# Iterated attention: a Newton step on GpSimd, another VectorE order, and a rearranged end

## What is computed

```python
q, k, v = heads(xn @ Wq + bq), heads(xn @ Wk + bk), heads(xn @ Wv + bv)   # 16 heads of 64
q, k = layernorm(q, gamma, beta), layernorm(k, gamma, beta)               # over the 64 of a head
def step(carry, _):
    q_cur, converged = carry
    attn = softmax(einsum('bhqd,bhkd->bhqk', q_cur, k) / 8)
    out = einsum('bhqk,bhkd->bhqd', attn, v)
    diff = norm(out - q_cur)                  # one number over all of the tensor
    q_new = where(converged, q_cur, out)
    return (q_new, converged | (diff < 1e-4)), None
(q_final, _), _ = scan(step, (q, False), None, length=3)
x = x + merge_heads(q_final) @ Wo + bo + ffn(xn)
```

## Time and profile before

| | us |
|---|---|
| median of 3 runs (lowest, highest) | 3179.82 (3178.55, 3186.2) |
| the profiled execution | 3181.74 |
| its span, first to last instruction | 3180.4 |

### The profile page before, as it was taken

One profiled execution on the slowest core, in us unless ns is written; L12 is line 12 of the kernel. 1 busy time (PEld: TensorE's weight loads), 2 busy tenths in 40 slices (PEclk: granted clock), 3 DMA queues, 4 the chain that ended last, 5 costly groups with the idle time before them and its releaser, 6 DMA issues.

```text
span 3180.4 us, 72036 instructions
## 1 busy us (share of the span) xinstructions
PE 2905.9 (91%) x24663; PEld 2226.7 (70%) x24663; DVE 2526.8 (79%) x5836; ACT 2206.5 (69%) x6152; POOL 2012.5 (63%) x2045
## 2 busy tenths in 40 slices
PE   6999988886999979999979999999999999999997
PEld 4666555565788877897857777777777777777775
DVE  7788899569777764664578888888888888888886
ACT  4566666643555565465368888888888888888885
POOL 2633344223555555235068888888888888888884
PEclk7999999998999989999989999999999999999998
DMA  3222422000000011102000000000000000000000
GB/s 117 73 80 73 147 86 86 19 7 1 1 1 1 1 51 53 35 1 64 2 13 2 2 2 1 2 2 2 2 2 2 2 2 2 2 2 2 1 2 27
DMA packets 68871, 77.15 MB, mean 24 GB/s; under 512 B 8016, under 2 KB 60320, under 8 KB 68384
## 3 DMA queue, kind: packets, MB, share of 16 engines
q1 hardware_dynamic: 64912, 71.10, 7.3%
q10 hardware_dynamic: 3600, 1.46, 0.2%
HBM read 52.61 MB, written 18.87 MB: 22 GB/s over the span
## 4 chain that ended last, share of the span: by engine, by line
PE 38%; DVE 10%; POOL 8%; issue 5%; ACT 4%; DVEq 0%; POOLq 0%; ACTq 0%
PE psum L2562 9%; PE psum L2544 7%; PE psum L2526 6%; POOL attn_p L3024 4%; DVE attn_pt L2823 2%; DVE sb_few L2810 2%; PE psum L1908 2%; PE psum L1759 2%; ACT attn_p L2668 2%; PE psum L2001 2%; PE psum L1761 2%; PE psum L1760 2%; PE psum L2589 2%; PE psum L1808 2%; PE psum L2468 1%
## 5 line engine op out<-in xcount | busy, mean ns | idle before, releaser
L3024 POOL TENSOR_TENSOR attn_p<-attn_p,sb_few 128x512 f32<-128x512 f32 x768 | 797.3, 1052 | 174.1 <-DVE sb_few L2817 172.0
L2668 ACT ACTIVATE attn_p<-psum,sb_few 128x256 f32<-128x256 f32 x1536 | 721.1, 480 | 60.9 <-DVE sb_few L2810 60.8
L2810 DVE TENSOR_REDUCE sb_few<-psum 128x2 f32<-128x512 f32 x768 | 508.5, 680 | 12.1 <-PE psum L2526 6.7
L2544 PE MATMUL psum<-sb_kept,attn_p 128*128 128x128 f32 x3072 | 412.0, 277 | 33.1 <-DVE attn_pt L2823 29.2
L2562 PE MATMUL psum<-attn_pt,attn_v 128*64 128x256 f32 x3072 | 384.2, 387 | 30.7 <-DVE attn_pt L2823 30.7
L2544 PEld LDWEIGHTS psum<-sb_kept,attn_p 128*128 128x128 f32 x3072 | 335.7, 141 | 82.5 <-issue 30.4
L506 DVE TENSOR_REDUCE sb_a_nm<-psum 128x2 f32<-128x512 f32 x512 | 329.0, 685 | 64.9 <-PE psum L396 46.9
L572 ACT ACTIVATE sb_a_pt<-psum 128x512 f32<-128x512 f32 x512 | 278.8, 598 | 93.8 <-PE psum L403 65.5
L2668 ACT ACTIVATION_READ_ACCUMULATOR attn_p<-psum,sb_few 128x1 f32 x1536 | 318.9, 208 | 0.0
L2562 PEld LDWEIGHTS psum<-attn_pt,attn_v 128*64 128x64 f32 x3072 | 202.7, 136 | 156.9 <-issue 75.4
L2823 DVE COPY attn_pt<-psum 128x512 f32<-128x512 f32 x384 | 264.0, 688 | 34.0 <-PE psum L2544 29.8
(11 more groups left out here) (441 smaller groups left out, 7706.8 us busy)
## 6 DMA issues: line engine op xcount, KB each, us to landing
sb_a_spread<-a_spilled SPq DMA_DIRECT2D x64, 256.0 KB, 3.0
a_spilled<-sb_a_part_hi SPq DMA_DIRECT2D x64, 128.0 KB
a_spilled<-sb_a_part_lo SPq DMA_DIRECT2D x64, 128.0 KB
sb_a_spread<-a_spilled SPq DMA_DIRECT2D x64, 128.0 KB, 3.2
sb_gate_up<-in_L_ffn_Wg SPq DMA_DIRECT2D x32, 128.0 KB
sb_gate_up<-in_L_ffn_Wu SPq DMA_DIRECT2D x32, 128.0 KB
sb_down_w<-in_L_ffn_Wd SPq DMA_DIRECT2D x32, 128.0 KB, 2.5
sb_x<-in_L_attn_x SPq DMA_DIRECT2D x4, 512.0 KB, 7.6
```

The source lines that it names most:

```text
L2544: mm = pe.transpose(PT(e)[:, kt * N + t * P:kt * N + (t + 1) * P], Pr[p % 3][:, e, t, kt * P:(kt + 1) * P], c.ident)
L2668: ins = act.activation(Pr[p % 3][:, e, t, :], S(p, e)[:, t * N:(t + 1) * N], ACT.Exp, bias=nm[:, p % 4, e, t:t + 1], accum_out=rsum[:, p % ...
L2810: dve.tensor_reduce(nm[:, p % 4, e, :], S(p, e).rearrange("p (t n) -> p t n", t=TB), AX.X, ALU.max, negate=True).then_inc(maxed.sem, 1)
L3024: pool.tensor_tensor(P3, P3, spread(rinv[:, p % 4, e, :], N), ALU.mult).then_inc(normed[e].sem, 1)
```

## The change

- **Newton.** For u+1 = 1 to 31 the step moves from DVE to POOL (four 128x16 instructions, each waiting for the one before), `newton(u+1, 0)` in round 3 ahead of two `scale`, `newton(u+1, 1)` in round 4 ahead of a `differ` and a `scale`. Unit 0 keeps it on DVE.
- **DVE's order.** `variance(u+1, 0)` moves from the end of round 2 to round 3 between the first two `maxima`. `sum_squares(u+1, 2)` and `step_end(u, 0)` take the places that newton leaves. `step_end(u-1, 2)` moves behind `invert(a, 1)`. `invert(a+1, 0)` comes ahead of `low(b)`. `add_bias(u+2, 0)` moves between the two `low` of round 5.
- **ACT and POOL.** `first_high(u, 1)` moves from the start of round 0 to the end of round 5; `differ(u, 0, 0)` from the start of round 4 to the middle of the last two norms of round 3.
- **The end.** The squared moves are summed a round or more earlier, the flags are made in rounds TURNS-1 and TURNS+1, the predicated copies are spread through the last rounds, `turn_y` begins ahead of the last output projection, the first four of eight pieces go by an ACT copy and a POOL addition, the others by DVE as before, and there are eight stores of 256 KB.

```diff
@@ -2565,13 +2570,12 @@
...
                 pe.wait_ge(*totalled(s))
-                if s == 0:
-                    pe.wait_ge(*y_kept(STEPS * (NU - 1) + 1))
+                pe.wait_ge(*y_kept(STEPS * (NU - 1) + s))
                 pe.matmul(M[:, 0:1], c.ones, tot[:, s:s + 1], start=True, stop=True).then_inc(all_summed.sem, 1)
             def out_product(u, s):
-                if s == 2 and u + 1 == NU:
-                    pe.wait_ge(*flagged(0))
+                if s and u + 1 == NU:
+                    pe.wait_ge(*flagged(s - 1))
                 elif s == 2 and u + 2 < NU:
...
+            def turn_y(n):
+                pe.wait_ge(*chosen(4 if n == 7 else n // 2))
+                if n >= 4:
+                    pe.wait_ge(*y_copied(n - 4))
+                for m in range(4):
+                    k = 4 * n + m
+                    mm = pe.transpose(bank_of(n)[:, m * P:(m + 1) * P], xnT[:, k * P:(k + 1) * P], c.ident)
+                mm.then_inc(turned_y.sem, 1)
+
             for n in range(6):
...
@@ -2604,30 +2617,26 @@
...
                 if turning:
-                    turn(p + 1, 1)
-                    turn(p + 1, 0)
+                    turn(p + 1, int(r <= TURNS))
+                    turn(p + 1, int(r > TURNS))
+                if r == TURNS + 1:
+                    total(1)
+                if turning:
                     weigh(p)
...
                 behind_weighing(u, i)
+                if r == TURNS - 1:
+                    total(0)
                 if r < TURNS:
...
                     out_product(u, 1)
-                if r == TURNS + 1:
-                    total(0)
-            total(1)
-            for g in range(4):
-                pe.wait_ge(*chosen(g))
-                for half_ in range(2):
-                    for m in range(4):
-                        k = 8 * g + 4 * half_ + m
-                        mm = pe.transpose(c.banks[2 * (g % 2) + half_][:, m * P:(m + 1) * P], xnT[:, k * P:(k + 1) * P], c.ident)
-                    mm.then_inc(turned_y.sem, 1)
-                if g == 1:
-                    pe.wait_ge(*result(0))
-                elif g == 2:
-                    pe.wait_ge(*result(1))
+                if r == TURNS + 2:
+                    turn_y(0)
+                    turn_y(1)
+            for n in range(2, 8):
+                turn_y(n)
...
@@ -2763,6 +2775,13 @@
...
                 behind_keep(u, i)
+            for n in range(4):
+                act.wait_ge(*turned_y(n))
+                if n == 0:
+                    act.wait_ge(*normed[0].all())
+                    act.wait_ge(*turned[0].all())
+                    act.wait_ge(*turned[1].all())
+                act.copy(y_copy(n), bank_of(n)).then_inc(y_copied.sem, 1)
...
+                    dve.wait_ge(*varied(2 * u))
                 dve.tensor_reduce(ss[:, n % 2, :], sq[:, n % 2, :].rearrange("p (h d) -> p h d", d=HD3), AX.X,
...
                 dve.wait_ge(*summed(4 * u + 2 * n + 1))
+                if u:
+                    dve.wait_ge(*refined(2 * u + n - 1))
                 dve.tensor_scalar(v_[:, :, :], ss[:, :, :], 1.0 / HD3, 1e-5, ALU.mult, ALU.add).then_inc(varied.sem, 1)
-            def newton(u, n):
-                dve.wait_ge(*rooted(2 * u + n))
+            def newton_first(n):
+                dve.wait_ge(*rooted(n))
                 own(dve.scalar_tensor_tensor(t_[:, :, :], v_[:, :, :], -0.5, rs[:, :, :], ALU.mult, ALU.mult))
...
@@ -2879,46 +2902,54 @@
...
             def choose(n, g):
-
-                cols = slice(g * 8 * P, (g + 1) * 8 * P)
-                m = flag[:, n:n + 1].to_broadcast((P, 8 * P))
+                cols = slice(g * 8 * P, ((g + 1) * 8 - (2 if n and g == 3 else 0)) * P) if g < 4 else slice(T - N, T)
+                m = flag[:, n:n + 1].to_broadcast((P, cols.stop - cols.start))
                 return dve.copy_predicated((yT[1], xnT)[n][:, cols], m, yT[n][:, cols])
...
                 dve.tensor_scalar(flag[:, 0:1], tot[:, 0:1], 1e-8, None, ALU.is_lt).then_inc(flagged.sem, 1)
-                dve.wait_ge(*flagged(0))
-                dve.wait_ge(*y_kept(STEPS * (NU - 1) + 1))
+
+            def flag_second():
+                dve.wait_ge(*all_summed(1))
+                dve.tensor_scalar(flag[:, 1:2], M[:, 0:1], tot[:, 0:1], 1e-8, ALU.min, ALU.is_lt).then_inc(flagged.sem, 1)
...
                     split_q(u, 0)
+                elif i == 3 and u + 1 < NU:
+                    variance(u + 1, 0)
             def behind_second_maxima(u, i):
-                if i == 0 and u:
+                if i == 0 and 0 < u < NU:
                     step_end(u - 1, 1)
+                elif u == NU and i == 0:
+                    dve.wait_ge(*flagged(0))
+                    choose(0, 0)
+                elif i == 5 and u + 1 == NU:
+                    total(0)
                 elif i == 4 and u + 1 < NU:
...
             def behind_third_maxima(u, i):
-                if u + 1 < NU and i in (3, 4):
-                    newton(u + 1, i - 3)
+                if i == 3 and u + 1 < NU:
+                    sum_squares(u + 1, 2)
+                elif i == 4 and u < NU:
+                    step_end(u, 0)
...
                     add_bias(u + 1, 1)
-                if i == 3 and u:
-                    step_end(u - 1, 2)
-                elif i == 4 and u < NU:
-                    step_end(u, 0)
...
                 if u + 1 < NU:
-                    if i in (1, 2):
-                        add_bias(u + 1, i + 1)
-                    if i in (1, 2, 3):
-                        sum_squares(u + 1, i - 1)
+                    if i == 1:
+                        add_bias(u + 1, 2)
+                        sum_squares(u + 1, 0)
+                    elif i == 2:
+                        sum_squares(u + 1, 1)
+                        add_bias(u + 1, 3)
...
@@ -2945,8 +2974,20 @@
...
                 behind_third_maxima(u, i)
+                if r == TURNS:
+                    step_end(NU - 1, 1)
+                elif r == TURNS + 1:
+                    choose(0, 1)
+                    total(1)
+                    c.dve_own(choose(0, 2))
                 if turning:
                     move_odd(b + 1)
+                if r == TURNS + 1:
+                    flag_second()
+                    dve.wait_ge(*flagged(1))
+                    choose(1, 0).then_inc(chosen.sem, 1)
+                    dve.wait_ge(*y_kept(STEPS * (NU - 1) + 1))
+                    c.dve_own(choose(0, 3))
                 behind_second_odd(u, i)
...
                     split_q(u, 1)
-                if turning:
-                    low(b)
+                elif i == 3 and 0 < u < NU:
+                    step_end(u - 1, 2)
                 if rising:
...
                 if turning:
+                    low(b)
+                if u + 2 < NU and i == 5:
+                    add_bias(u + 2, 0)
+                if turning:
                     low(b + 1)
-                if i == 2 and u + 1 < NU:
-                    variance(u + 1, 0)
                 if rising:
...
                 behind_inverses(u, i)
-                if r == TURNS + 1:
-                    total(0)
+                if r == TURNS - 1:
                     flag_first()
-                    choose(0, 0)
-                    choose(0, 1)
-                elif r == TURNS + 2:
-                    choose(0, 2)
-            own(choose(0, 3))
-            total(1)
-            dve.wait_ge(*all_summed(1))
-
-            own(dve.tensor_scalar(flag[:, 1:2], M[:, 0:1], tot[:, 0:1], 1e-8, ALU.min, ALU.is_lt))
+                elif r == TURNS + 1:
+                    choose(1, 1).then_inc(chosen.sem, 1)
+            choose(1, 2).then_inc(chosen.sem, 1)
+            choose(1, 3).then_inc(chosen.sem, 1)
+            step_end(NU - 1, 2)
             dve.wait_ge(*y_kept.all())
-            choose(1, 0).then_inc(chosen.sem, 1)
-            for g in range(4):
-                if g < 3:
-                    choose(1, g + 1).then_inc(chosen.sem, 1)
-                for half_ in range(2):
-                    dve.wait_ge(*turned_y(2 * g + half_))
-                    xs = x[:, 8 * g + 4 * half_:8 * g + 4 * half_ + 4, :]
-                    ins = dve.tensor_tensor(xs, xs, c.banks[2 * (g % 2) + half_].rearrange("p (t d) -> p t d", d=D), ALU.add)
-                ins.then_inc(result.sem, 1)
+            choose(1, 4).then_inc(chosen.sem, 1)
+            for n in range(4, 8):
+                dve.wait_ge(*turned_y(n))
+                dve.tensor_tensor(x_of(n), x_of(n), bank_of(n), ALU.add).then_inc(result.sem, 1)
...
@@ -2999,6 +3032,14 @@
...
+            def newton(u, n):
+                own = c.pool_own
+                pool.wait_ge(*rooted(2 * u + n))
+                own(pool.tensor_tensor(t_[:, :, :], rs[:, :, :], rs[:, :, :], ALU.mult))
+                own(pool.tensor_tensor(t_[:, :, :], v_[:, :, :], t_[:, :, :], ALU.mult))
+                own(pool.tensor_scalar(t_[:, :, :], t_[:, :, :], -0.5, 1.5, ALU.mult, ALU.add))
```

(27 more changed lines are left out.)

## The result

The changed kernel takes 3155.36 us (median; 3151.76 to 3160.22), the kernel before beside it 3179.19 us. The ratio is 0.992, with a 95% interval of 0.9908 to 0.9933: 24 us, or 0.8%, faster. Predicted were 3158.0 us and faster. The total is met, but two of its terms are not: the steady part gave 7.0 us more than the forecast and the end 4.3 us less, about half of it. That the total lies within 2.6 us of the forecast is therefore partly luck.

What follows compares the result with a forecast made beforehand. DVE's newton was taken to hold PE in round 4, POOL's norms at the turn into round 1. Gains of 13.5 us (odd units 15 x 0.9, even none) and 8.5 (end) sum to 22.0: 3158.0 us, range 3145 to 3174.

Steps and rivals of the forecast that it cites:

- PE's wait in round 4: PE's 0.97 us wait for DVE's `move_odd` before the second `weigh` shrinks to nothing, worth 0.9 on PE.
- Newton's price: Newton on POOL in rounds 3 and 4: four dependent instructions at 0.30 us each, 1.2 per newton.
- (b): Rival: POOL pays more for newton, 0.42 us per instruction, giving 3181, or 3166 half way; chance 0.13.
- (d): Rival: slower, POOL bounds every unit; 3209 at 2.15 us per newton, 3194 at 1.9; chance 0.10.
- `variance` loses a race of 0.04: Round 3: `variance` starts 0.04 us behind POOL's `square`, waits for its end, shifts the reciprocal by 0.95, costs POOL 0.58.
- (a): Rival: `variance` wins the race in round 3; even units gain 0.54 us as well, 3149; chance 0.18.
- POOL's walk: POOL's starts through rounds 3 and 4: the next scale stays at 2419.00, the whole room of 2.88 us used.
- Odd units: POOL's idle before two norms leaves its queue 0.65 and 1.39 us; each odd unit gains 0.9 (0.6 to 1.1).
- If that cover went, 0.4 per unit: `step_end(u-1, 2)` moved: `turn_p` waits for `scale` till 2406.5, covered as PE has until 2407.08; costed at nothing.
- The end: After the last norms: copies moved earlier, additions shared, a smaller last store; gain 8.5 us (6 to 12).
- the waiting case: At the end, predicated copies wait for POOL: `weigh` until 3159.1, copies until 3168.3, end at 3172.4; otherwise 3169.
- POOL busy per even unit: Sign: POOL near 45.3 us busy per even unit, with PE waiting for norms in rounds 0 and 1.

Runs made afterwards that it cites:

- e1: The changed kernel with `variance(u+1, 0)` back at the end of round 2, all else the same; 3142.2 us.
- e2: The changed kernel with both newton steps back on DVE behind the third maxima, the other moves kept; 3223.2 us.
- e8: The changed kernel with `variance(u+1, 0)` back in round 2 and the newton of round 3 back on DVE, that of round 4 on POOL; 3166.9 us.
- e4: The changed kernel with the first of newton's four POOL instructions done three times; 3187.3 us.
- e7: The changed kernel without ACT's copies and POOL's additions at the end: DVE adds all eight pieces, stored in order 0 to 7; 3153.2 us.
- e12: e1 with `low(b)` again ahead of `invert(a+1, 0)` on DVE; 3144.8 us.

## Why the prediction came out, point by point

**PE's wait in round 4: right.** 0.9 was expected to go, and 30.7 us became 0.2. Between PE's first turns of rounds 4 and 5 the time fell from 9.35 to 8.37. Along POOL's norms round 4 shrank only from 8.98 to 8.31, and these 8.31 are POOL's own instructions without a stop.

**Newton's price: right.** 0.30 a step was taken from a neighbour 128x32 and its idle; measured are starts 0.29 to 0.31 apart and means of 204 to 222 ns. The far ends (b) and (d), with POOL small instructions at 0.42 or 0.54 a step, did not come. The rule of the Trainium skill cited there, GPSIMD Engine Reference, "Engine selection", decides wrongly here: a 128x16 instruction takes 0.16 to 0.18 on DVE (e1, e2, e8) and 0.22 on POOL when nothing is in its way, but on DVE beside a busy POOL it took 0.6 to 1.2 (e2, e8).

**`variance` loses a race of 0.04: right.** It took 1.03, as `split_q` had suggested. Rival (a) was what would have followed had it won, and two units at 94.7 were to be its sign. Two units came out at 94.89, nearer to that than to the forecast's 95.3, but not by (a)'s mechanism. e1 takes the race away: it gains 0.78 per pair, where (a) had 0.54, in the even unit alone.

**POOL's walk: right, a little pessimistic.** It had POOL without a stop from the first norm of round 3 to the end of round 4, using up its whole 2.88 of room and ending where it used to. The trace shows the same sequence without a stop, ending about 0.2 us earlier. The step: I let the whole shift of 0.95 reach the reciprocal, which before stood 0.75 behind the start of `move_odd` and now stands 0.60 behind it (2386.64 to 2387.24), so 0.15 of the shift went into a wait that was there. Hence even units gain 0.22 instead of 0.0.

**Odd units: the size right (1.10 for 0.9), the reason half wrong.** I gave them slack on POOL's queue that would swallow `variance` and a dearer newton. e1 and e4 show that it swallows little: 0.34 of 0.44 and 1.03 of 1.22 arrive. The failed step is to subtract idle time of POOL in round 5 from a loss in rounds 2 to 4. The loss has reached PE before the slack comes. One handover is seen in the rows: `turn_p` waits for `scale` in round 3 of both parities, 0.35 in the changed kernel, 0.94 in e4, under 0.1 in e1. The prediction had looked at this place ("PE has until 2407.08"; "If that cover went, 0.4 per unit") and put it at nothing; the cover went. In round 4, where the changed kernel loses another 0.2 to e1, PE shows no idle time before the turn, and by which handover that loss passes is open. What sets odd units apart is `split_q`: round 5 went from 9.07 to 8.21, and `split_q` from 1.80 (behind a `differ`) to 1.16 (ahead of it). The prediction named that as a side effect, "frees DVE of up to 1.0", and it is the difference between the parities: 0.86 in this round, against 0.88 in all.

**The steady sum:** 13.5 forecast, 20.5 measured. The even units, forecast at nothing, gave 4.0 (0.22 each, 0.93 in unit 30), and the odd ones 16.5 for 13.5. Terms mis-sized; the mechanism that the forecast rests on, PE's wait for newton, is the one that the runs show.

**The end: right in its course, wrong in its last two terms.** Counted in the time of before (the first norms of the last units laid on each other), the waiting case had `weigh` end at 3159.1, `low` at 3161.5 and the last copy at 3168.3. Measured were 3158.8, 3161.0 and 3168.6. Copies and POOL exclude each other, as e7 shows by taking POOL away. The Trainium skill says so in SBUF — State Buffer, "SBUF: two separate sides" (an exclusive lock for the whole instruction), and the trace agrees. Then two terms fail. From the last copy to the last addition I counted 1.5, a turn and one addition; all four of DVE's additions stood behind the copies, and it took 2.4, so the last addition ended at 3170.9 instead of 3169.8, and not before 3170, which the prediction had set as a sign of being wrong. And the store was to take 2.6 of the 3.45, being "half as large", while "eight DMA issues instead of four cost nothing: they are spread over 8 us". Six of the eight pieces were issued between 3143.5 and 3146.8 (an issue took up to 0.87 us), moved one after another at 0.9 us each, and the end came 5.16 us after the last addition. A store alone did take no longer than forecast (2.30); what failed is the "nothing" for those in front of it. That is 2.6 us, and with the 1.1 of the additions the 3.7 that lie between the walk's 8.0 and the measured 4.3; the other 0.5 was put on top of the walk, as the forecast took 8.5. I had looked at when the results were made on average, not at when they become free to store at the end. What POOL's additions do to the copies the waiting case had right (3.6 us, from 3164.7 to 3168.3; e7 shows 3.4), but it never weighed them against additions by DVE alone, which end 1.6 us sooner (e7).

**POOL busy per even unit:** 45.3 forecast, 44.52 measured; the 0.08 between dependent instructions counts as idle, not busy. It blocks POOL all the same. The sign named with it, PE waiting for norms in rounds 0 and 1 of the even units, is faint: PE waits for a norm once in the stretch shown, 0.2 us.

**The end of e1** is 0.75 us longer than that of the changed kernel, with the same instructions (22.21 to 21.46; e2, e8 and e12 have 22.3). The clock is what differs: their last `weigh` ended 1.1 to 1.2 us later. Copy (1,1) then starts 0.37 us later against the last norm and stands 0.13 instead of 0.48 behind the start of POOL's first addition, so that it waits longer for it and takes 2.34 instead of 1.97. The order of these two starts is a race of its own: in e4 both start in the same hundredth (3171.47), the copy takes 1.32 and POOL's addition 2.44, and with `weigh` as late as in e1 the end is 1.0 us shorter (21.20). The clock is no term of the prediction's end. What stays open is why it fell in some traces and not in others.

## What to carry to other kernels

Before a small instruction is placed on DVE, look at what POOL runs at that moment: its price is its own 0.17 us or what is left of POOL's instruction, and a few hundredths of start decide; moving it by one place can be worth more than moving it to another engine. Room on an engine counts only if it lies before the point where the next engine takes the result: compare the loss with the spare time at each handover (0.23 us between a norm's end and PE's turn here, and none at `scale`), not with the idle sums of a unit. At the end of a program cost the stores from the moment when the last results come in a bunch, at the rate at which they move (0.9 us per 256 KB here). Look at the granted clock of each stretch before two ends are compared. And test each part of a combined change alone: here one of the parts was worth as much as the whole.

## What the runs showed of the hardware that was not expected

- The exclusion works both ways and in the order of starts: `split_q` 0.58 us ahead of `differ` makes POOL wait (1.74 for 1.28), 0.03 behind makes DVE wait (1.82 for 1.17). Predicated copies of 128x1024 take part: 1.3 us alone, 2.0 to 2.4 beside POOL's additions, which grow from 1.27 to 2.3.
- A `tensor_scalar` on 128x16 with one input waits as the ones with two inputs do (1066 ns in the mean of 64 in the changed kernel; 0.16 us in e1, where it starts 0.05 before a norm ends). The section of the Trainium skill named above (SBUF — State Buffer, "SBUF: two separate sides") has two-input instructions and a mode with two ports as the ones that need the shared pair; which of them this one is, no row shows.
- 256 KB stores on one queue, issued as fast as it takes them: the issue grows from 0.37 to 0.87 us and they land one every 0.9 us (e7). On two queues in turn the issue stays at 0.37 to 0.40, but the pieces together still move at 249 to 298 GB/s, and the end comes only 0.6 us closer to the last addition (4.03 against 4.62).
- The same instructions, behind the same idle times of PE, ran at a granted clock of 1.00 in one trace and of 0.50 in another (the last `weigh`), which moved the end of the program by 0.5 to 1.1 us.
